# Graph network on one core: ScalarE's Abs in place of TensorE's flips, a bound that raises the products, other columns for layer 0 and other table stores

## What is computed

```python
msg = concat([h[src], h[dst]], axis=1) @ WM + bM
s    = segment_sum(msg, dst);  mean = s / deg
mean_sq = segment_sum(msg * msg, dst) / deg
mx, mn = segment_max(msg, dst), segment_min(msg, dst)
agg  = concat([mean, mx, mn, std, var, s], axis=1)
hu   = concat([h, agg, agg * amp, agg * att], axis=1) @ WU + bU
hbn  = batchnorm(hu / sqrt(n));  hm = leaky_relu(hbn @ Wmix + bmix)
h    = relu(batchnorm(hm + h)) + h
```

## Time and profile before

| | us |
|---|---|
| median of three runs | 3894.86 |
| profiled execution, its own time | 3899.44 |
| its span, first to last instruction | 3897.3 |
| TensorE matmul busy | 3282.0 (84%), 29640 matmuls |
| VectorE busy | 3138.2 (81%) |
| GpSimd busy | 2246.3 (58%) |
| ScalarE busy | 1169.8 (30%) |

### The profile page before, as it was taken

One profiled execution on the slowest core, in us unless ns is written; L12 is line 12 of the kernel. 1 busy time (PEld: TensorE's weight loads), 2 busy tenths in 40 slices (PEclk: granted clock), 3 DMA queues, 4 the chain that ended last, 5 costly groups with the idle time before them and its releaser, 6 DMA issues.

```text
span 3897.3 us, 88696 instructions
## 1 busy us (share of the span) xinstructions
PE 3282.0 (84%) x29640; PEld 2057.8 (53%) x29640; DVE 3138.2 (81%) x6027; ACT 1169.8 (30%) x3428; POOL 2246.3 (58%) x2221
## 2 busy tenths in 40 slices
PE   0054599999989799999988799999987899999986
PEld 0022355455448566555667466565566465555575
DVE  6599589899878788888876788888876788888875
ACT  4302022222215322222225332222235222222243
POOL 6401577777753157777750177777750277777650
PEclk9997899999999899999999999999998999999998
DMA  7002678788882255555670356556660455566740
GB/s 213 17 0 75 223 262 274 267 280 285 292 296 92 92 168 175 185 178 182 205 242 15 120 177 184 171 182 196 205 206 4 146 185 171 177 188 193 224 155 34
DMA packets 237856, 675.58 MB, mean 173 GB/s; under 512 B 83074, under 2 KB 100310, under 8 KB 234758
## 3 DMA queue, kind: packets, MB, share of 16 engines
q1 hardware_dynamic: 126439, 426.27, 32.7%
q0 software_dynamic: 78400, 192.26, 17.1%
q10 hardware_dynamic: 32732, 54.15, 3.9%
HBM read 523.47 MB, written 153.60 MB: 174 GB/s over the span
## 4 chain that ended last, share of the span: by engine, by line
PE 25%; issue 20%; POOL 13%; DMA 12%; DVE 11%; ACT 2%; SPq 1%; DVEq 1%; ACTq 0%; POOLq 0%
POOL rows L883 12%; PE bank L1817 10%; DMA rows<-table,lists 9%; PE bank L1791 5%; PE bank L1884 4%; DVE accL L1440 2%; PE bank L1800 2%; DVE scr L1363 2%; DVE scr L1374 1%; SPq L478 1%; PE bank L1872 1%; DMA left<-accL 1%; DVE accL L1436 1%; POOL accL L926 1%; DMA RE<-ohd 1%
## 5 line engine op out<-in xcount | busy, mean ns | idle before, releaser
L883 POOL DMA_INDIRECT rows<-table,lists x1828 | 1854.1, 1014 | 760.7 <-issue 514.6
L1817 PE MATMUL bank<-RE,split 125*64 125x482 bf16 x15600 | 1833.1, 369 | 45.8 <-ACT scr L607 45.7
L1817 PEld LDWEIGHTS bank<-RE,split 125*64 125x64 bf16 x15600 | 948.0, 110 | 705.7 <-ACT scr L607 51.6
L634 ACT ACTIVATE split<-rows,masks 128x128 f32<-128x128 f32 x1828 | 602.3, 391 | 1658.9 <-DMA rows<-table,lists 1251.1
L1791 PE MATMUL bank<-RE,split 126*64 126x482 bf16 x7800 | 913.4, 369 | 40.7 <-DVE scr L1374 21.4
L1363 DVE TENSOR_TENSOR scr<-scr,bank 128x964 f32<-128x964 f32 x624 | 693.2, 1111 | 86.4 <-PE bank L1791 79.7
L1374 DVE TENSOR_TENSOR scr<-scr,bank 128x964 f32<-128x964 f32 x624 | 692.9, 1110 | 50.7 <-PE bank L1800 44.8
L1791 PEld LDWEIGHTS bank<-RE,split 126*64 126x64 bf16 x7800 | 470.4, 110 | 380.3 <-DVE scr L1374 38.0
L1800 PE MATMUL bank<-RE,flip_w 126*64 126x482 bf16 x2600 | 388.7, 371 | 83.8 <-DVE scr L1361 45.9
L1435 DVE TENSOR_TENSOR accL<-accL,rows 128x192 f32<-128x192 f32 (+2 forms) x664 | 225.5, 340 | 270.5 <-DMA rows<-table,lists 267.5
L1440 DVE TENSOR_TENSOR accL<-accL,split 128x384 f32<-128x384 f32 (+2 forms) x664 | 344.5, 519 | 1.7
(11 more groups left out here) (282 smaller groups left out, 2750.4 us busy)
## 6 DMA issues: line engine op xcount, KB each, us to landing
RE<-ohd SPq DMA_DIRECT2D x395, 602.5 KB
RE<-by_chunk SPq DMA_DIRECT2D x130, 602.5 KB
ohd<-RE SPq DMA_DIRECT2D x130, 602.5 KB, 4.9
rows<-table,lists POOLq DMA_INDIRECT x1828
left<-accL POOLq DMA_DIRECT2D x20, 1280.0 KB, 7.4
dense_d<-scr ACTq DMA_DIRECT2D x104, 241.0 KB
split<-dense_d ACTq DMA_DIRECT2D x16, 625.0 KB, 6.5
table<-accL SPq DMA_DIRECT2D x36, 250.0 KB
```

What stands on the lines that cost most here:

```text
L634: ins = nc.scalar.activation(masked_rows[:, g % GM_RING * GC + k, :], ring[:, b * GC + k, :], ACT.Copy, scale=masks[:, m:m + 1])
L883: nc.gpsimd.indirect_dma_start(ring[:, b * GC + k, :], None, table, bass.IndirectOffsetOnAxis(ap=lists[:, c:c + 1], axis=0)).then_inc(col_ ...
L1817: ins = nc.tensor.matmul(SB[h * D:(h + 1) * D, 0:CH], split[0:NP, k, q, h * D:(h + 1) * D], columns_of(k, NP), start=k == 0 and q == 0, st ...
```

## The change

- `flips` is gone from TensorE. ScalarE's `turn_blanks` takes the absolute value of each quad's two PSUM banks in place (964 columns, f32), between `greatest(i)` and `least_of(i)`. The blank becomes positive by this, so all real values must be positive: a bound is computed at each layer's start and added to every product through partition 126 of the one-hot columns, which is now always one (`compare` takes the maximum with `always`), and taken off again in `cross_halves` and `merge_halves`.
- The bound: VectorE takes the greatest of h (`heights`, filled by a new form of the last step), TensorE multiplies it by the negative weights (`bound_down`), VectorE reduces the row, SyncE copies it into the split (`raise_rows`), TensorE and VectorE make `lower` from it. The first quad's sums come before its products in chunk 0, so that this runs beside them. In layer 0 two more operations and a reduction over h (3125 columns) stand ahead of `t_ps`, on which the blank rows wait.
- Blank rows are written to one partition for the first part and two for the others (before: one each).
- ScalarE's queue in the dense stage is now by quads: Abs, then at chunk 0's last three quads one of the three clears each, at the first quad of a later chunk `evacuate` and `cross_halves`, at the third `store_chunk`, then the masks due in the quad. The weight loads stay ahead of all of it.
- Columns run over steps 100 to 622 in layer 0 and 56 to 634 in the others.
- Table stores: seven DMAs of 112 partitions (both halves at once) and one of the other 13, in place of 14 of 125.
- ScalarE does all seven pieces of the last ReLU, VectorE the additions with the greatest taken in the same instruction. ScalarE's program has layer 0 written out ahead of its loop.
- `update`: one h matmul of 128 columns first, in place of two of 64 at the end.

```diff
-COL_SPAN = (56, 622)
+COL_SPAN = (56, 634)
+FIRST_SPAN = (100, 622)
...
-                for a in range(2):
-                    sp.dma_start(table3[:, a * HALF + j0:a * HALF + j0 + n, :], T[0:NP, a, j0:j0 + n, :]).then_inc(S["tab_st"], 16)
+                sp.dma_start(table4[0:MOST, :, j0:j0 + n, :], T[0:MOST, :, j0:j0 + n, :]).then_inc(S["tab_st"], 16)
+                if m == BATCHES - 1:
+                    sp.dma_start(table4[MOST:NP, :, :, :], T[MOST:NP, :, :, :]).then_inc(S["tab_st"], 16)
...
+            def raise_rows(l):
+                wait(sp, "raise_v", l * RAISING + 3)
+                sp.dma_start(split[NP + 1:NP + 2, :, 0, 0:2 * D],
+                             raise_row[:, :].unsqueeze(1).to_broadcast([1, TILES, 2 * D])).then_inc(S["raise_st"], 16)
...
+                def turn_blanks(c, i):
+                    n = (l * NCH + c) * QUADS
+                    wait(act, "g_top", n + i + 2)
+                    got = QB[i % QRING] if i < QUADS - 1 else PAIR[:, 0:CH]
+                    nc.scalar.activation(got, got, ACT.Abs).then_inc(S["g_abs"], 1)
...
                 load_weights(l)
-                clear_sums()
                 for c in range(NCH):
...
+                    for i in range(QUADS):
+                        turn_blanks(c, i)
+                        if c == 0 and i >= QUADS - 3:
+                            clear_sums(i - QUADS + 3)
+                        if c > 0 and i == 0:
+                            evacuate(c - 1)
+                            cross_halves(c - 1)
+                        if c > 0 and i == 2:
                             store_chunk(c - 1)
+                        for g in due.get(i, []):
+                            if g == 0 and span is FIRST_SPAN:
+                                act.wait_ge(S["listed"], 4)
+                            mask_group(g)
...
-                for r in STEPS[0:3]:
+                for r in STEPS:
                     nc.scalar.activation(OT[:, r], OT[:, r], ACT.Relu, bias=c_bias, scale=c_scale).then_inc(S["r_done"], 1)
...
+            nc.vector.tensor_scalar(fallers[:, :, :], WAB[:, :, :], -MARGIN, 0.0, ALU.mult, ALU.max)
+            step(nc.vector.memset(heights[:, :], 0.0))
+            dve.wait_ge(S["h0_ev"], HALF)
+            step(nc.vector.tensor_reduce(heights[:, 0:1], hT[:, :], AX.X, ALU.max))
             nc.vector.nop().then_inc(S["t_ps"], 1)
...
-                    wait_at(dve, "g_flip", n + i + 1)
+                    wait_at(dve, "g_abs", n + i + 1)
...
-                    nc.vector.tensor_scalar(BK[b], VB[g % 2], answers, None,
-                                            ALU.is_equal).then_inc(S["cmp"], 1)
+                    nc.vector.tensor_scalar(BK[b], VB[g % 2], answers, always,
+                                            ALU.is_equal, ALU.max).then_inc(S["cmp"], 1)
...
+                        if first and i == 0:
+                            wait(pe, "raise_v", (l + 1) * RAISING)
+                            wait(pe, "raise_st", l * 16 + 16)
...
-                    def flips(i):
-                        wait_at(pe, "g_top", n + i + 2)
-                        for k in steps_of(i):
-                            ins = nc.tensor.matmul(pair_bank(i, k)[half(k), 0:CH], flip_w[0:NP + 1, :], columns_of(k, NP + 1),
-                                                   start=False, stop=True, skip_group_check=True)
-                        ins.then_inc(S["g_flip"], 1)
...
+                    if first:
+                        arrived(0)
+                        sums(0)
+                        bound_up()
                     for i in range(QUADS):
                         products(i)
-                        if i > 0:
+                        if i > (1 if first else 0):
                             sums(i - 1)
```

More of the change, by code:

```diff
@@ L235, in build @@
         (c_nmu, c_std, c_rstd, c_scale, c_bias, c_zb, c_sum, c_sq, c_about, c_off, c_slope, c_var, c_shift_u, c_shift_o,
-         tiny, epsc, oneh, kb, answers, none, least, most) = (col[:, k:k + 1] for k in range(22))
+         tiny, epsc, oneh, kb, answers, none, least, most, always, lower, height) = (col[:, k:k + 1] for k in range(25))
         n_all, n_quart = float(FC), FC / 4
@@ L592, in _, with layer @@
                 nc.scalar.copy(V[:, r], VI[:, r]).then_inc(S["v_ev"], 1)
-            with act.Fori(0, LAYERS) as l:
+            def layer(l, span):
                 def turned(m):
@@ L811, in _ @@
                 wait(act, "aff2", l + 1)
-                for r in STEPS[0:3]:
+                for r in STEPS:
                     nc.scalar.activation(OT[:, r], OT[:, r], ACT.Relu, bias=c_bias, scale=c_scale).then_inc(S["r_done"], 1)
+            layer(0, FIRST_SPAN)
+            with act.Fori(1, LAYERS) as l:
+                layer(l, COL_SPAN)
         @block.gpsimd
@@ L1453, in dense @@
                 def dense(n0):
-                    due = columns_at()
-                    begin, end = COL_SPAN
-                    opened = quad_of(min(group_at(g) for g in range(len(LEAD), NG)))
+                    span = FIRST_SPAN if numbers else COL_SPAN
+                    due = columns_at(span)
+                    begin, end = span
+                    opened = quad_of(min(group_at(g, span) for g in range(len(LEAD), NG)))
                     compared = [2]
@@ L1770, in half, with arrived @@
                         return slice(D * (k % 2), D * (k % 2) + D)
-                    def products(i):
+                    def arrived(i):
                         if first and i % 2 == 0:
@@ L1808, in sums @@
                             wait_at(pe, "s_evac", l * NCH + c + 1)
-                        blocks = list(steps_of(i))
-                        middle = len(blocks) // 2
-                        used_up = False
-                        for o, k in enumerate(blocks):
-                            if o == middle:
-                                flips(i)
+                        for k in steps_of(i):
                             for q in range(3):
@@ L1880, in update @@
                         wait(pe, "hut_ev", i - 1)
+                    if a == 0:
+                        both = UPS[j % 2][0:NP, 0:384].rearrange("p (a s) -> p a s", a=2)[:, :, 0:D]
+                        nc.tensor.matmul(both, hT[:, j * NP:(j + 1) * NP], W[:, W_U0:W_U0 + P], start=True, stop=False, skip_group_check=True)
                     wait(pe, "at_ev", 2 * i + a + 1)
```

155 lines of the change are left out of this document (88 added, 67 removed).

## The result

The changed kernel takes 4000.39 us (median of 4 runs, 3988.74 to 4006.95) against 3893.67 for the kernel before (4 runs, 3887.85 to 3898.64): a ratio of 1.0272, with a 95% interval of 1.0256 to 1.0288. It is slower by 2.7%, where 0.4% was forecast, and 4000 lies far outside the range of 3872 to 3942. The profiled execution took 3997.34 us with a span of 3995.3, 98.0 us longer than the span before.

A forecast was written before the change was run, and what follows sets the result against it. From each layer's 14th gather on, GpSimd's gathers were taken to set the pace. Waits -12, layers 1 to 3 first joins +26.3, layer 0 +10, node stage -8 gave +16.3 us: 3910, 0.4% slower, range 3872 to 3942.

The forecast's parts named there:

- The four more ReLU pieces: ScalarE at the start of layers 1 to 3: they move its start by 2.5 us, bounds 0 and 2.5.
- Layer 0 behind its 14th gather: Layer 0's stretch from 14th to last gather: 634.1 us before, 17 us shorter through fewer waits.
- Of the 20 us of waits I leave 3: GpSimd's waits behind layer 0's 14th gather: 20.1 us before, 3 left.
- `compare` with a second pointer: VectorE's compare with a second operand: put at nothing, as VectorE has 10% to spare in layer 0.
- Rival E: VectorE's compare leaves its fast rate: +1.9 us x 130 = 250 us, 60 absorbed in layer 0, total 4100; chance 3%.
- Layer 0's first join: Start of layer 0, through stores, weight loads, Abs and chunks 0 and 1: 522 against 488.81, +33 us.
- Layers 1 to 3, first join: Layer starts, with the first Abs behind 25 weight loads: 14th gather later by 12.1, 9.1 and 5.1 us, sum +26.3.
- Waits behind it in layers 1 to 3: GpSimd's waits behind the 14th gather: 6.8, 4.6 and 4.9 us fall to 1.4 each, -12 us.
- The tail: Last gather's end to node stage: layer 0's 46.2 us shrinks to 40; layers 1 to 3 given no change from 37.5.
- Node stage: The node stage with one 128-column h matmul in place of two: -8 us in all, bounds 0 and 12.
- The stores in layers 1 to 3: Table stores by 112 partitions: table lands some 10 us earlier, worth nothing since it ends before the first Abs.
- B: Layer 0's eight stores still block ScalarE 4.6 us each; first Abs and later steps 27 us later, 3937; chance 15%.

The follow-up runs named there:

- the stack: The changed kernel with columns from steps 56 and 46, the evacuation ahead of the next chunk's first Abs, and late weight loads: 3795.65 us, 0.9777.
- the second run: The changed kernel with the evacuation of a chunk's sums moved ahead of the next chunk's first Abs on ScalarE: 3950.84 us, 1.0162.
- the fastest kernel: The stack with its compare back at one operand and the raising row's ones written once into each one-hot buffer: 3782.52 us, 0.9728.

## Why the prediction was wrong in size, and which steps failed

Right: GpSimd paces each layer from its 14th gather (undoing the span moved start and end alike, and the flips were worth 30 us of 269); slower, and by the start of the layers; the first Abs stands behind the weight loads (VectorE waits 31.8 us for it in layer 0). That in layers 1 to 3 it comes 39.5 to 40.3 us behind the layer's first matmul, where 39.4 to 39.6 was worked out, is luck: two terms were wrong and cancel. The four more ReLU pieces moved nothing (layer 1's first weight load is issued 18.0 us behind the first matmul, where it was 18.6 and 21.1 was forecast), and the 25 loads took 21.4 to 21.7 us where 18.3 was carried over:
```profile
1393.25 0.52 ACTq L696 DMA_DIRECT2D W<-in_WM  x1
...
1414.40 0.54 ACTq L707 DMA_DIRECT2D W<-in_bM  x1
1415.16 1.82 ACT L648 ACTIVATE bank<-bank 128x964 f32<-128x964 f32 x2 [21.75 <-issue]
```
Of the prediction's own signs, two of being right came true (the first Abs within 0.3 us of the last load's end, TensorE's share of 89% in mid-layer) and three did not (the 14th gather 5 to 12 us later, waits under 3 us, 522 in layer 0). One of being wrong came true, more than 10 us of waits behind the 14th gather: 34.9 in layer 0 and 10.5 in layer 1. Its reading, that VectorE and ScalarE between them set the pace, holds for these waits, not for the stretch: gathers and their gaps fill the other 574 to 628 us.

The steps, forecast against measured:

- **Layer 0 behind its 14th gather: -17 forecast, +28 measured.** The largest error, 45 us: 32 of it waits, 14 longer gathers. "Of the 20 us of waits I leave 3" took it that a faster TensorE ends waits. It ends none in layer 0: 22.8 us stayed in the kernel before when its flips went, and 20.6 with the evacuation ahead. The other 14 of the 34.9 are the evacuation's, since TensorE stands 4 to 10 us at each chunk's boundary; the stretch as a whole became 9.3 us shorter by that move. GpSimd waits in them for VectorE's additions; why 17 to 24 us of waits remain in layer 0 of every kernel whose evacuation stands behind no Abs stays open. And "`compare` with a second pointer" was put at nothing, because VectorE had 10% to spare. The row to look at was another engine's: the gathers, which are on the path. The runs put it at 11 to 23 us, about 20 (+20 in the kernel before; -23 in layer 0 of the changed one, -11 by its ratios; -15.7 and -19 in the stack). Rival E named the compare, but as VectorE's own time.
- **Layer 0's first join: 522 forecast, 542.03 measured.** The stores took 16.6 us for 10, from 388.9 on. The weight loads took 24.4 for 18.3: their price was read in layer 1 of the kernel before. Then chunk 0 lasted 51.1 us from the first Abs's end to VectorE's copy at 481.99, and 51.0 were forecast. Chunk 1 took 54.1 in place of the 46.5 of TensorE's matmuls: TensorE begins its sums 2.7 us into it, behind the evacuation, then takes 3.0 longer for the first 36 matmuls at the lower clock, and at the chunk's end VectorE does 2.6 us of list copies and masks ahead of step 100.
- **Layers 1 to 3, first join: +12.1, +9.1, +5.1 forecast, +13.1, +18.4, +12.9 measured.** Layer 1 was right, by the two terms above that cancel. For the others I carried over layer 1's 55.2 us from Abs to 14th gather; they took 63.9 and 63.4. The evacuation explains 5.7 and 4.7 us (the second run). The rest is about as long as a pause of VectorE ahead of chunk 1's first maximum, 4.1 and 4.0 us in layers 2 and 3 against 0.3 in layer 1, in which it waits for nothing that the profile shows. The kernel before has it too (3.7 and 4.4 against 0.3), so its trace could have told; what causes it stays open. Layer 2, before and after:
```profile
2229.36 1.16 DVE L1361 COPY scr<-bank 128x964 f32<-128x964 f32 x1 [3.73 <-issue]
```
```profile
2329.57 1.16 DVE L1421 COPY scr<-bank 128x964 f32<-128x964 f32 x1 [4.09 <-issue]
```
- **Waits behind it in layers 1 to 3: 1.4 us each forecast, 10.5, 9.9 and 9.0 measured.** Again the evacuation: with it ahead the waits are 3.6, 2.5 and 2.9 us, and the three stretches are 6 to 7 us shorter.
- **The tail: nothing forecast for layers 1 to 3, -11.7 us measured** (3.8, 4.9 and 3.0). A gain that I had missed; in layer 0 -6.7 for -6. I made no run for its cause.
- **Node stage: -8 forecast, -13 measured** (3.5, 3.7, 3.7, 2.1), a gain just past the bound of 12.
- **The stores in layers 1 to 3: nothing forecast, and not shown for the changed kernel.** The first gather comes 9 to 11 us earlier (27.8 to 28.7 us behind the first matmul for 37.6 to 39.1), and the wait for the Abs hides whatever else they give. In the kernel before, where nothing hides it, the 14th gather goes 4 to 8 us earlier by them, so "worth nothing" is true only behind the weight loads. Over the whole kernel before they are worth 36 us, 20 or so of it in layer 0's first join. The forecast had that gain folded into a later first join.

The sum: layer 0's first join 20, its stretch 45, the other first joins 18, their stretches 16, less 12 for tails and 5 for the node stage, is 82: just what lies between the +16.3 forecast and the +98.0 measured. The range failed because it was built from the rivals' prices, one at a time (B, at 15%, gave 27 us), while the misses had one sign. Most were places where I had let ScalarE's or VectorE's new work count only on its own engine; the 17 us of waits taken off layer 0 for a faster TensorE were not, and no row had shown that TensorE made them.

## What to carry to other kernels

When work moves to an idle engine, its busy share says nothing; list what stands ahead of it in that engine's queue at each place where somebody will now wait for it, and move those (loads, evacuations) first. Here two such moves were worth 43 and 80 us, and the Abs itself some 6 to 16. And where a queue of DMAs issued by one engine sets the pace, cost each edit of a neighbour by what it does to that engine's instructions, not by its own time.

## What was not expected of the hardware

A gather that starts beside a compare is held. From the changed kernel's timeline, GpSimd and VectorE:
```profile
705.23 0.94 POOL L926 DMA_INDIRECT rows<-table,lists  x1 [0.30 <-issue]
...
706.33 0.91 DVE L1461 TENSOR_SCALAR RE<-RE,col 128x2410 bf16<-128x2410 bf16 x1
...
706.48 1.58 POOL L926 DMA_INDIRECT rows<-table,lists  x1 [0.30 <-issue]
...
710.29 0.91 DVE L1461 TENSOR_SCALAR RE<-RE,col 128x2410 bf16<-128x2410 bf16 x1
...
710.43 2.06 POOL L926 DMA_INDIRECT rows<-table,lists  x1 [0.30 <-issue]
...
712.79 0.94 POOL L926 DMA_INDIRECT rows<-table,lists  x1 [0.30 <-issue]
```
Alone it takes 0.94 us, beside a compare 1.58 or 2.06. Over layer 0's stretch the gathers that overlap a compare take 1.21 us on the mean in the kernel before and 1.31 us with the second operand alone, the others 1.00 and 1.02 (111 compares lie in each of the two stretches). The Trainium skill ("SBUF — State Buffer", section "SBUF: two separate sides") says that a VectorE instruction in a mode that uses both port pairs locks GpSimd out, so that GpSimd can't write the descriptors of its DMAs until the instruction ends; the trace agrees in kind. By that rule a compare longer by 56 ns would cost at most 130 times that, an estimate of 7 us; the runs show 16 to 22 us in the gathers, so what more the second operand does stays open.

The price of a DMA issue on ScalarE's queue is not a constant: 25 weight loads took 18.3 us in layer 1 of the kernel before, 21.4 to 21.7 in layers 1 to 3 of the changed one and 24.4 in its layer 0, and the same eight stores took 16.6, 12.3 and 19.1 us in three kernels (the changed one, the one with late loads, the kernel before with the new stores). The granted clock of TensorE in layer 0's stretch went from 0.99 to 0.90 where it waited at each boundary, and was 0.96 in the fastest kernel.
